# Attention and routed experts on one core: the second list of routed tiles sorted by token tile, and five of eight result chunks finished while the last 24 routed tiles run

## The reference

```python
x = x + attn(layernorm(x))          # causal; q, k, v of 1024 features as one head
x = x + ffn(layernorm(x))           # 8 experts, each token goes to 2 of them

# ffn, x: [4096, 128]
scores = softmax(x @ gate_w.T)
top_scores, sel = top_k(scores, 2)
order = argsort(sel.T.reshape(-1), stable=True)        # 8192 choices, sorted by expert
x_sorted = x[order % N]
y = (silu(x_sorted @ w1[e]) * (x_sorted @ w3[e])) @ w2[e]   # e: the expert of the row
out = zeros.at[order % N].add(y * score_of_the_choice)
```

## Time and profile before

| | |
|---|---|
| median of 3 runs | 285.78 us (284.77 to 285.9) |
| span of the profiled execution | 326.4 us; its time outside the span is not shown |
| PE busy | 252.2 us, 77% of the span |
| DVE busy | 206.5 us, 63% |
| POOL busy | 191.3 us, 59% |
| ACT busy | 126.1 us, 39% |
| moved by DMA | 28.92 MB |

### The profile page before, as it was taken

The page is one execution under the profiler, slowest core; times in us unless marked ns, Lnnn a source line. Parts: engine busy times, 40 slices in busy tenths (PEclk is TensorE's granted clock), DMA queues, the critical chain, the costliest instruction groups (busy, mean ns, idle before and its releaser), DMA issues.

```text
span 326.4 us, 5986 instructions
## 1 busy us (share of the span) xinstructions
PE 252.2 (77%) x1618; PEld 205.5 (63%) x1619; DVE 206.5 (63%) x889; ACT 126.1 (39%) x347; POOL 191.3 (59%) x257
## 2 busy tenths in 40 slices
PE   1889999999898999886864376998989898988000
PEld 1767888788667777765742265876767676776000
DVE  1448888676987577863831355675757666666175
ACT  1136665564565546622620112443434343333000
POOL 2437756887888887766377473554545554646100
PEclk9999999999999999999795585999999999999555
DMA  7952112110010111142122121443222222221499
GB/s 228 320 161 65 38 62 77 50 41 27 20 33 33 50 44 35 35 99 71 41 74 66 41 76 49 104 110 84 70 77 69 70 82 65 80 62 43 149 351 294
DMA packets 31111, 28.92 MB, mean 89 GB/s; under 512 B 4328, under 2 KB 25840, under 8 KB 31088
## 3 DMA queue, kind: packets, MB, share of 16 engines
q1 hardware_dynamic: 22512, 17.49, 19.2%
q0 software_dynamic: 4352, 9.05, 8.2%
q10 hardware_dynamic: 4224, 2.10, 2.1%
HBM read 16.40 MB, written 12.22 MB: 88 GB/s over the span
## 4 chain that ended last, share of the span: by engine, by line
PE 56%; POOL 9%; issue 8%; another core or an unknown queue 7%; DVE 7%; DMA 6%; ACT 4%; SPq 1%; POOLq 0%; DVEq 0%
PE scores L490 7%; PE weighed L543 7%; PE weighed L605 5%; PE scores L582 5%; PE scores L584 5%; PE turned L591 5%; POOL expert_rows L396 4%; PE mixed L605 4%; PE scores L583 4%; PE turned L517 4%; DMA XX<-choice_rows 3%; PE scores L574 2%; PE mixed L504 2%; DMA X<-L_attn_in_features 2%
## 5 line engine op out<-in xcount | busy, mean ns | idle before, releaser
L405 POOL DMA_INDIRECT choice_rows<-ysb,ydest x72 | 68.9, 957 | 61.1 <-DVE ysb L942 42.0
L396 POOL DMA_INDIRECT expert_rows<-rows,slots x64 | 65.4, 1022 | 20.1 <-issue 16.1
L714 ACT ACTIVATE sil<-scores 128x256 f32<-128x256 f32 x72 | 27.6, 383 | 83.5 <-PE scores L584 56.3
L582 PE MATMUL scores<-W,xTh 128*128 x72 | 36.6, 508 | 11.4 <-issue 6.1
L922 DVE CAST xTh<-scores 128x128 fp32r<-128x128 f32 x72 | 20.8, 289 | 34.6 <-PE scores L574 19.9
L591 PE MATMUL turned<-identf,g 128*128 128x128 f32 x144 | 29.4, 287 | 13.0 <-DVE g L932 12.7
L543 PE MATMUL weighed<-TL,PT 128*128 128x128 f32 x288 | 38.0, 277 | 1.8 <-DVE X L789 1.8
L490 PE MATMUL scores<-XX,TL 128*128 128x512 f32 (+3 forms) x96 | 36.8, 492 | 1.0 <-ACT TL L694 1.0
L543 PEld LDWEIGHTS weighed<-TL,PT 128*128 128x128 f32 x288 | 34.7, 192 | 2.1 <-issue 2.1
L719 ACT ACTIVATE gTs<-turned 128x256 f32<-128x256 f32 x72 | 27.6, 383 | 21.1 <-PE turned L591 16.2
L591 PEld LDWEIGHTS turned<-identf,g 128*128 128x128 f32 x144 | 18.1, 145 | 22.9 <-DVE g L932 16.4
(11 more groups left out here) (132 smaller groups left out, 528.6 us busy)
## 6 DMA issues: line engine op xcount, KB each, us to landing
xt<-expert_rows SPq DMA_DIRECT2D x72, 66.0 KB
XX<-choice_rows SPq DMA_DIRECT2D x16, 256.0 KB, 5.0
ysb<-L_ffn_w SPq DMA_DIRECT2D x16, 128.0 KB, 2.2
out<-X ACTq DMA_DIRECT2D x8, 256.0 KB, 5.7
choice_rows<-ysb,ydest POOLq DMA_INDIRECT x72
X<-L_attn_in_features SPq DMA_DIRECT2D x2, 512.0 KB, 9.4
expert_rows<-rows,slots POOLq DMA_INDIRECT x64
expert_rows<-padrows SPq DMA_DIRECT2D x1, 528.0 KB
```

Of the source, the lines that this page charges most:

```text
L396: nc.gpsimd.indirect_dma_start(xs, bass.IndirectOffsetOnAxis(ap=slots[:, u, k:k + 1], axis=0), rows[:, u % ROWS_RING, k, :], None).then_in ...
L405: nc.gpsimd.indirect_dma_start(yb, bass.IndirectOffsetOnAxis(ap=ydest[:, q:q + 1], axis=0), ysb[:, q, :], None).then_inc(y_out[q], 16)
L582: mm(bank[2 + j % 2], xTh[:, j % 2, :], hi, start=True, stop=False)
L714: copy(sil[:, j % 2, :], bank[2 + j % 2][:, 0:H], ACT.Silu).then_inc(sil_rdy, 1)
```

## The change

The second list is no longer in order of expert alone. It has 16 segments (`SEG`): first, for each of the 8 experts, the tiles that hold rows of the first 20 query tiles and are not in the first list, then, for each expert, the rest. So all rows of the first 20 query tiles are in routed tiles 0 to 47 (`NT0 + NEAR`). The tables of the list get 16 columns in place of 8 (`past` and `pasts` 640 elements in place of 320), and there is one instruction more in the parts `list_rest(1)` and `list_rest(4)` each.

The first 20 query tiles are token tiles 0 to 17, 24 and 25, five chunks: 0 to 3, 4 to 7, 8 to 11, 12 to 15, and 16, 17, 24 and 25. The other three are 18 to 21, then 22, 23, 26 and 27, then 28 to 31 (`CHUNKS`; `pieces` gives their runs of neighbouring tiles). Twelve more iotas on GpSimd write the destinations for this order.

SP reads chunks 0 to 3 right after it issued the load of tile 57, once the stores of tiles 0 to 47 are done. VectorE adds one choice of one chunk after each of its steps 60 to 69. After the last load SP writes chunks 0 to 4 as they are added and reads chunk 4 after the first write. After the last store SP reads the three chunks that are left; ScalarE issues their writes. The loops of VectorE and SP are shortened and the steps behind them written out: VectorE from step 50, SP from the load of tile 56.

```diff
+CHUNKS = [(0, 2), (4, 2), (8, 2), (12, 2), (16, 8), (18, 2), (22, 4), (28, 2)]
+N_EARLY = 5
+FETCH_AT, FINISH_AT = 57, 60
...
+def pieces(c):
+
+    a, apart = CHUNKS[c]
+    return [(a, FIN)] if apart == 2 else [(a, 2), (a + apart, 2)]
...
                     sp.dma_start(xt[:, j, :], xs[ds(r, P), :]).then_inc(xt_in[j], 16)
...
+                    if then is not None and j == then[0]:
+                        then[1]()
...
-            with sp.Fori(M0, M_TILES) as m:
-                load(m)
-
-
-            for q in range(OUT_LANES):
-                sp.wait_ge(y_out[q], 16 * len(range(q, NT, OUT_LANES)))
...
-            for c in range(ZF):
+            def fetch_first():
+
+                for q in range(OUT_LANES):
+                    sp.wait_ge(y_out[q], 16 * len(range(q, NT0 + NEAR, OUT_LANES)))
+                for c in range(ZF):
+                    fetch(c)
+
+            with sp.Fori(M0, FETCH_AT // LANES) as m:
+                load(m)
+            load(FETCH_AT // LANES, then=(FETCH_AT % LANES, fetch_first))
+            for m in range(FETCH_AT // LANES + 1, M_TILES):
+                load(m)
+
+
+            for c in range(N_EARLY):
+                sp.wait_ge(sum1, c + 1)
+                for n, z in pieces(c):
+                    sp.dma_start(ov[:, n:n + z, :], X[:, n:n + z, :]).then_inc(out_done, 16)
+                if c + ZF < N_EARLY:
+                    fetch(c + ZF)
+
+            for q in range(OUT_LANES):
+                sp.wait_ge(y_out[q], 16 * len(range(q, NT, OUT_LANES)))
+            for c in range(N_EARLY, NF):
                 fetch(c)
...
+            def list_rest(part):
+
+                t, segments = slice(NT0, NT), range(SEG)
+                if part == 0:
+                    v.tensor_tensor(pad0[:, :], cnt[:, 1, :], stretch0[0:1, :], ALU.add).then_inc(pad0_rdy, 1)
+                    whole_tiles(1, P - 1)
+                elif part == 1:
+                    link(v.tensor_copy(base[:, E:SEG], ntf[:, 0, :]))
+                    link(v.tensor_tensor(new[:, :], ntf[:, :, :].rearrange("p a e -> p (a e)"), base[:, 0:SEG],
+                                         ALU.subtract))
+                    link(v.tensor_tensor_scan(cum[:, 1:], new[:, :], zeros[:, :], 0.0, ALU.add, ALU.add))
+                elif part == 2:
+                    passed(NT1, segments, base)
+                elif part == 3:
+                    totals(t, segments)
...
+            def add_choice(c, k):
+
+                a, apart = CHUNKS[c]
+                Xc = pairs[:, a // 2:a // 2 + apart // 2 + 1:apart // 2, :]
+                if k == 0:
+                    dve.wait_ge(yf_in[c % ZF], 16 * K * (c // ZF + 1))
+                else:
+                    dve.wait_ge(sum0, c + 1)
+                v.tensor_tensor(Xc, Xc, yf[:, c % ZF, k, :, :].rearrange("p (n t) d -> p n (t d)", t=2),
+                                ALU.add).then_inc([sum0, sum1][k], 1)
...
+            with dve.Fori(1, (NT0 + NEAR) // OUT_LANES) as r:
                 for q in range(2, OUT_LANES + 2):
                     tile_step(r, q)
...
+            for t in range(NT0 + NEAR + 2, NT):
+                tile_step(t // OUT_LANES, t % OUT_LANES)
+                if FINISH_AT <= t < FINISH_AT + K * N_EARLY:
+                    add_choice((t - FINISH_AT) // K, (t - FINISH_AT) % K)
```

More of the change, by code:

```diff
@@ L136, in build @@
         cnt, cnti, ntiles = sb("cnt", [1, 2, E]), sb("cnti", [1, 2, E], i32), sb("ntiles", [1, 2, E], i32)
[L137 to L140, removed]
+        ntf, zeros = sb("ntf", [1, 2, E]), sb("zeros", [1, SEG])
+        cum = sb("cum", [1, SEG + 1])
+        taken = sb("taken", [1, E + 1])
+        base = sb("base", [1, SEG + 1])
+        new, jump, step = (sb(n, [1, SEG]) for n in ("new", "jump", "step"))
         pad0 = sb("pad0", [1, E], i32)
         iotat = sb("iotat", [1, NT])
-        past, pasts = sb("past", [1, NT, E]), sb("pasts", [1, NT, E])
+        past, pasts = sb("past", [1, NT1 * SEG]), sb("pasts", [1, NT1 * SEG])
         e_of, s_of, i_of, r_of = (sb(n, [1, NT]) for n in ("e_of", "s_of", "i_of", "r_of"))
@@ L192, in build @@
         sum0, sum1, out_done = sem("sum0"), sem("sum1"), sem("out_done")
-        N_CONST, N_PADS, M_TILES = 6 + K, 10, NT // LANES
+        N_DESTS = 1 + sum(len(pieces(c)) for c in range(FIN, NF))
+        N_CONST, N_PADS, M_TILES = 6, 11 + K * N_DESTS, NT // LANES
+        ov = out.rearrange("b (i p) d -> p (b i) d", p=P)
         def is_tile(u):
@@ L283, in _, with load @@
                          padrows[:, E:, :]).then_inc(padded, 16)
-            def load(m, pads=()):
+            def load(m, pads=(), then=None):
                 _, firsts = nc.values_load_multi_w_load_instructions(
@@ new lines, in whole_tiles, with passed @@
+            def whole_tiles(l, above):
+                link(v.tensor_scalar(cnti[:, 0:l + 1, :], cnt[:, 0:l + 1, :], float(above), None, ALU.add))
+                link(v.tensor_scalar(ntiles[:, 0:l + 1, :], cnti[:, 0:l + 1, :], P.bit_length() - 1, None,
+                                     ALU.logical_shift_right))
+                link(v.tensor_copy(ntf[:, 0:l + 1, :], ntiles[:, 0:l + 1, :]))
+            def passed(n, segments, first):
+                m = len(segments)
+                past_ = past[:, 0:n * m].rearrange("p (t e) -> p t e", e=m)
+                pasts_ = pasts[:, 0:n * m].rearrange("p (t e) -> p t e", e=m)
+                v.tensor_tensor(past_, cum[:, 1:m + 1].unsqueeze(1).to_broadcast([1, n, m]),
+                                iotat[:, 0:n].unsqueeze(2).to_broadcast([1, n, m]), ALU.is_le)
+                link(v.tensor_tensor(jump[:, 0:m], first[:, 1:m + 1], first[:, 0:m], ALU.subtract))
+                link(v.tensor_tensor(step[:, 0:m], jump[:, 0:m], new[:, 0:m], ALU.subtract))
+                link(v.tensor_tensor(pasts_, past_, step[:, 0:m].unsqueeze(1).to_broadcast([1, n, m]), ALU.mult))
@@ new lines, in list_full @@
+            def list_full(part):
+                t, experts = slice(0, NT0), range(E)
+                if part == 0:
+                    whole_tiles(0, 0)
+                elif part == 1:
+                    link(v.tensor_tensor_scan(cum[:, 1:E + 1], ntf[:, 0, :], zeros[:, 0:E], 0.0, ALU.add, ALU.add))
+                    link(v.tensor_scalar(cum[:, 1:E + 1], cum[:, 1:E + 1], float(NT0), None, ALU.min))
+                    link(v.tensor_tensor(new[:, 0:E], cum[:, 1:E + 1], cum[:, 0:E], ALU.subtract))
+                    link(v.tensor_copy(base[:, 0:E], new[:, 0:E]))
+                elif part == 2:
+                    passed(NT0, experts, taken)
@@ L954, in tile_step @@
                     weighted(r, q - 2)
+                elif isinstance(r, int) and r >= 1:
+                    weighted(r - 1, q + OUT_LANES - 2)
                 if more:
```

105 lines of the change are left out of this document (48 added, 57 removed).

## The result

The changed kernel took 287.91 us in the median of 4 runs (287.1 to 289.57), the kernel before 285.27 us beside it: ratio 1.0111, 95% interval 1.0082 to 1.0141. It is 2.6 us **slower**, where 2 us faster was forecast. Two more comparisons gave 1.0085 [1.006, 1.011] and 1.0098 [1.0064, 1.0133].

The account below looks back on a forecast made before the run. It took TensorE to bound the routed tiles until 302 us and transfers the tail. Tail −8.8, loads +2.8, clock +1.65, additions +1.8 and list +0.6 gave about −2.0 on 285.78: 283.8 us, range 279.2 to 288.6.

Parts of the forecast that it names:

- SP's new wait for the stores up to tile 47 costs about nothing: SP before the early reads: tile 57's load already waits for tile 49's product, stores finish 2.7 us after starting; no cost.
- Loads behind the early reads: SP's queue, served in order: TensorE waits +2.8 us for tile 58's load behind eight reads; bounds 0 and 3.8.
- Clock: TensorE after the wait for tile 58: one 3.3 us stretch at half clock, +1.65 us; bounds 0 and 10.2.
- Ten additions: VectorE in tiles 60 to 69: 0.61 us each, partly hidden in idle time, +1.8 us, midway between 0.5 and 3.2.
- The row of L901: Trace row cited against contention: L901, two SBUF operands, ran beside GpSimd's L396 in 0.47 us, so nothing is lost.
- Tail: After the last store: three chunks left where eight were, −8.8 us; bounds −8 and −10.
- Second list: VectorE during tiles 8 to 16: 16 segments instead of 8, 1.8 us of work mostly hidden, +0.6 us; bounds 0 and 1.8.
- No long steps without the profiler: Rival, chance 0.15: tile loop's long steps absent in unprofiled runs, the change gives back all it earns, +0.4, 286.2 us.
- The additions are paid in full: Rival, chance 0.11: VectorE becomes the bound in tiles 60 to 69, additions cost 6.1 instead of 1.8, 288.1 us.
- GpSimd blocks additions: Rival, chance 0.05: each VectorE addition waits for half of GpSimd's L396, +4.8 on the sum, 288.6 us.
- All hidden: Rival, chance 0.16: loads pass the early reads and long steps hold the additions, −7.7, 278.1 us.
- The clock stays low: Rival, chance 0.08: TensorE, waiting for VectorE, stays at 1.2 GHz, +6.6, 292.3 us.

Follow-up runs that it names:

- wait_alone: Kernel before, with SP also waiting for the stores of tiles 0 to 47 behind the load of tile 57, no early reads: 287.1 us, ratio 1.0079.
- reads_fast: Kernel before, plus eight 256 KB reads of the input behind the load of tile 57, no wait for stores; shorter-pace set: 288.15 us, ratio 1.011.
- adds_fast: Kernel before, plus ten unneeded 128x512 additions on VectorE in steps 60 to 69; shorter-pace set: 287.84 us, ratio 1.0091.
- list_only: Changed kernel without early chunks: new list and destinations kept, all eight chunks done after the last store: 283.78 us, ratio 0.9985.
- before_fast: Kernel before, unchanged, timed and profiled again in the third set, at the shorter pace: 284.42 us.
- adds_alone: Kernel before, plus ten unneeded 128x512 additions on VectorE in steps 60 to 69; first set, longer pace: 322.74 us, ratio 0.992.
- spread_late: spread62 with only chunk 0 added in the tile loop, chunks 1 to 4 after the last step, ScalarE issuing all writes: 318.67 us, ratio 0.9789.
- spread62: Changed kernel, early reads in four pairs behind loads of tiles 62, 64, 66, 68, additions from step 62: 276.91 us, ratio 0.9749; longer pace 314.99 us, 0.9709.
- before_again: Kernel before, unchanged, timed again in the first set for a second trace, at the longer pace: 326.44 us.

## Why the prediction was wrong, by its own steps

**The step that failed** is "SP's new wait for the stores up to tile 47 costs about nothing". It took the time of the store to be that of the product. In the runs GpSimd reaches that store 7 to 8 us after VectorE has written its rows; SP stood 5.8 us, and everything that the prediction itself had named as queued behind it (the loads, then TensorE) stood too. wait_alone shows it by itself: this wait, without a read or an addition, costs 2.4 us net. In the changed kernel, where the reads behind it had already used up the lead of the loads, it costs TensorE its full 5.8 us.

**Loads behind the early reads: +2.8, measured +3.7** (reads_fast). The mechanism, a queue served in order, was right, and so was the lead of 6.4 us; the reads took 10.1 us and not the 9.2 of the tail. The bound of 3.8 held.

**Clock: +1.65, measured +1.95.** Right, and one stretch only, as charged. It lasted 10.2 us by the granted clock (235.9 to 246.1), but TensorE stood for the first 6 of them, so the bound of 10.2 us of cost was far off.

**Ten additions: +1.8, measured +1.3 and +0.4.** In the changed kernel they cost 1.3 us up to the last `ysb` and 0.4 more in the last store. The size is near, but by luck: 1.8 was a midpoint between cases that both leaned on long steps or the lack of them. I had taken VectorE's own work in a step to be 1.24 us, from 0.23 of idle time. Its step with an addition is 1.65 us with no idle time, and the addition holds 0.60 of it (251.39 to 251.99), so the work is 1.05 and 0.42 were free; an addition lengthens VectorE's step by 0.18 and not by 0.38. The part on GpSimd's side I put at nothing, and where GpSimd is behind it is the larger one (3.5 us at the last store of adds_fast). Chunk 4's reads, which were to land in time, kept VectorE 0.33 us (at 265.18). The row of L901 misled me: there GpSimd's L396 starts at 187.13, ahead of the addition, and a store that starts first loses nothing. The next row of GpSimd in the same trace starts 0.23 us behind L905, and is longer:

```profile
188.39 1.10 POOL L396 DMA_INDIRECT expert_rows<-rows,slots  x1 [0.31 <-issue]
```

**Tail: −8.8, measured −9.3.** Right: 11.3 us from the first read to the end, against "some 12".

**Second list: +0.6, measured about 0** (list_only 0.9985). Its two products take 0.80 and 0.81 us against the forecast 0.85, and no cost of them shows.

**The rivals.** "No long steps without the profiler" was right that most of them are absent in the runs that count, and its 286.2 us came nearer than mine; but its cause was wrong (a pace that comes with a set of runs, not with the profiler: before_fast, profiled at the shorter pace, has a span of 282.2 us), and it had no wait for stores either. "The additions are paid in full" was right that VectorE becomes the bound of its own steps in tiles 60 to 69, at 0.18 us an addition and not 0.61. "GpSimd blocks additions" had the right pair of engines and the wrong loser. "All hidden" fell with the 9.46 us stall. "The clock stays low" did not happen: the granted clock is 1.00 from 246.2 to 267.

The measured 287.9 lies inside the range; the side was wrong. The measured terms are −9.3 (tail) + 5.8 (wait for stores) + 3.7 (reads) + 1.95 (clock) + 1.3 (additions) − 1.0 (last store, whose backlog was worked off) = +2.45. (The 1.0 is 1.4 of backlog that GpSimd worked off, less the 0.4 of the additions.) Without the wait for stores, the one term that the prediction put at about nothing, they would be some −3.3; but part of the backlog was worked off in that wait.

**What stays open**: why a set of runs has one pace or the other, why at 325 us adds_alone was faster and spread_late slower than spread62, and what the changed kernel itself does at that pace, where it was not run.

## What to carry to other kernels

Before you let a queue wait for another engine's output, read when that engine gets to the instruction, not when its input is ready: here GpSimd's rows all said 0.30 idle, the sign that it was behind, and its backlog cost nothing until someone waited for it. Work that goes ahead of a just-in-time load on the same queue should be handed out between the loads in small pieces (here 276.9 us for 280.2), and a stall of the bound engine costs less than its length while another engine uses it to catch up (5.2 us lost, 3.9 at the last store). To see what an added instruction costs, compare each step with the same step before, since long ones recur (here every eighth). If the profiled time and the median are 40 us apart, get a second profile before pricing anything from the first.

## What the runs showed of the hardware

- A GpSimd indirect store of 128 rows takes 0.96 us to issue. If it starts within 0.55 us behind the start of a 128x512 addition with two SBUF operands, it is longer by what is left of the 0.55: 1.34 us for most in adds_fast, 1.47 at most. If it starts first, both keep their length (0.96 and 0.68 us).
- Back to back, such stores are issued 1.26 us apart: 0.96 and 0.30 between.
- A load of 66 KB (128x132 floats) issued behind eight reads of 256 KB on SP's queue lands some 10.1 us after the first of them was issued.
- The same kernel has two paces, about 285 and 325 us, in sets of runs on one chip; from 205 to 250 us TensorE has 291 instructions in the one (before_fast) and 261 in the other (before_again), both at the full granted clock.
